# Other places in the line for scores, shifts, half-precision copies and value products in a decoder layer

## The reference

```python
scores = softmax(einsum('bhse,bhte->bhst', q, k) * scale, axis=-1)
att = einsum('bhst,bhte->bhse', scores, v)
x = layernorm(x + att.reshape(b, s, h * e) @ wo.T + bo)
# recurrence over t, elementwise in the 256 columns
out = A + exp(u + kk) * (vv * Bm + max(t - 1, 0))
A, Bm = exp(-w) * A + inc * exp(kk) * vv, exp(w) * Bm + inc * exp(-kk)
x = layernorm(x + out)
G, I = top_k(softmax(x @ Wg.T), 128)            # 128 of 128 tokens: all of them
h1 = gelu(ex @ W1[e] + b1[e])                   # 256 -> 1024
x = layernorm(x + sum_e G * (h1 @ W2[e] + b2[e]))
```

## Time and profile before

| | |
|---|---|
| median of 3 runs | 946.9 us (945.4 to 947.71) |
| the profiled execution, its own time | 947.15 us |
| its span, first to last instruction | 945.4 us |
| PE busy | 878.2 us, 93% |
| DVE busy | 596.7 us, 63% |
| ACT busy | 580.3 us, 61% |
| POOL busy | 79.1 us, 8% |
| granted clock of PE, mean | 0.968 of full speed |

### The profile page before, as it was taken

How to read it: one execution, slowest core, us unless ns; L and a number is a source line. 1 busy time by engine, 2 the same in 40 slices (tenths; PEclk the granted TensorE clock), 3 DMA queues, 4 the chain that set the end, 5 groups by cost and what they waited for, 6 DMA issues and landing times. The chain is left out here.

```text
span 945.4 us, 17487 instructions
## 1 busy us (share of the span) xinstructions
PE 878.2 (93%) x6480; PEld 799.0 (85%) x6480; DVE 596.7 (63%) x1222; ACT 580.3 (61%) x967; POOL 79.1 (8%) x116
## 2 busy tenths in 40 slices
PE   4759888899998999999998999999998999999997
PEld 3659888689987989888987899888997999899997
DVE  5888779767656575655676564664756555433574
ACT  4438875776657466665567666664666665445684
POOL 2320012000110010100120001200110000000000
PEclk8669989999999999999999999999999999999999
DMA  7617998998747954676547864578537765665340
GB/s 225 208 49 249 367 365 295 295 292 267 235 134 200 257 175 144 151 197 216 189 126 199 223 189 146 146 201 225 170 130 201 179 203 166 192 195 162 118 136 12
DMA packets 195379, 185.00 MB, mean 196 GB/s; under 512 B 61896, under 2 KB 161504, under 8 KB 195296
## 3 DMA queue, kind: packets, MB, share of 16 engines
q1 hardware_dynamic: 195296, 183.88, 65.0%
HBM read 135.60 MB, written 35.65 MB: 181 GB/s over the span
## 5 line engine op out<-in xcount | busy, mean ns | idle before, releaser
L881 ACT ACTIVATE h_all<-up_ps,b_all 128x512 f32<-128x512 f32 (+1 forms) x296 | 182.2, 631 | 246.4 <-PE up_ps L540 244.7
L775 PE MATMUL down_ps<-w_hi,h_hi 128*128 128x256 f32 x1024 | 297.4, 290 | 13.7 <-DVE acc L1124 13.6
L938 DVE TENSOR_TENSOR h_lo<-h_all,h_hi 128x512 fp32r<-128x512 f32 x256 | 177.2, 692 | 195.3 <-ACT h_hi L872 194.9
L776 PE MATMUL down_ps<-w_lo,h_hi 128*128 128x256 f32 x1024 | 292.0, 285 | 0.0
L777 PE MATMUL down_ps<-w_hi,h_lo 128*128 128x256 f32 x1024 | 291.7, 285 | 0.0
L538 PE MATMUL up_ps<-x2t_hi,w_hi 128*128 128x512 f32 (+1 forms) x592 | 221.8, 375 | 6.1 <-ACT h_all L881 5.2
L775 PEld LDWEIGHTS down_ps<-w_hi,h_hi 128*128 128x128 f32 x1024 | 197.4, 193 | 23.5 <-issue 12.5
L540 PE MATMUL up_ps<-x2t_hi,w_lo 128*128 128x512 f32 (+1 forms) x592 | 217.1, 367 | 0.0
L539 PE MATMUL up_ps<-x2t_lo,w_hi 128*128 128x512 f32 (+1 forms) x592 | 216.4, 366 | 0.0
L776 PEld LDWEIGHTS down_ps<-w_lo,h_hi 128*128 128x128 f32 x1024 | 198.2, 194 | 6.9
L777 PEld LDWEIGHTS down_ps<-w_hi,h_lo 128*128 128x128 f32 x1024 | 197.9, 193 | 0.0
(11 more groups left out here) (195 smaller groups left out, 958.7 us busy)
## 6 DMA issues: line engine op xcount, KB each, us to landing
w_hi<-w_parts SPq DMA_DIRECT2D x200, 256.0 KB, 3.3
w_lo<-w_parts SPq DMA_DIRECT2D x200, 256.0 KB, 3.6
w_raw<-in_w_dram SPq DMA_DIRECT2D x96, 256.0 KB, 4.2
w_parts<-w_hi SPq DMA_DIRECT2D x64, 256.0 KB, 4.0
w_parts<-w_lo SPq DMA_DIRECT2D x64, 256.0 KB, 4.4
x_in<-in_x_dram SPq DMA_DIRECT2D x8, 256.0 KB, 4.0
ctx_sb<-in_ctx_dram SPq DMA_DIRECT2D x8, 256.0 KB, 3.9
out_dram<-acc SPq DMA_DIRECT2D x8, 256.0 KB, 2.3
```

What stands on the lines that cost most here:

```text
L775: nc.tensor.matmul(ps, hi, w2h[:, c, :], start=c == 0 and j == 0, stop=False, skip_group_check=True)
L776: nc.tensor.matmul(ps, hi, w2l[:, c, :], start=False, stop=False, skip_group_check=True)
L881: a = nc.scalar.activation(h_all[:, unit % HALL, k * wide:(k + 1) * wide], up_ps[unit % 2][:, k * wide:(k + 1) * wide], ACT.Gelu_apprx_tan ...
L938: return nc.vector.tensor_tensor(dst, src, hi.bitcast(F32), ALU.subtract)
```

## The change

Numbers in `STEADY` and in the third pair's table of `EARLY` are changed; no code is. For pairs 3 to 7: T_0 and T_1 one item later, S_2 and S_3 two, M_2 three and M_3 four, so that the last two score steps stand at the last D of a visit and the shifts at the two items behind it; W_0, E_2 and E_3 two later, T_2 three, W_1 one, T_3 four, W_2 two, W_3 four, ATT two, CTX, WO, NORM1, Y1, XEXP and REC_0 to REC_3 one. BACK and what follows stay. For pair 2: T_0, T_1, M_3, W_0, W_1, T_2 and T_3 one later, W_2 and W_3 two.

```diff
-          V_ADD: -59, V_SPLIT: -58, S_0: -57, M_0: -57, S_1: -57, M_1: -57, DIAG_1: -53, E_0: -52, E_1: -52, T_0: -51, T_1: -46,
-          S_2: -45, M_2: -45, S_3: -45, M_3: -45, E_2: -40, E_3: -40, W_0: -40, T_2: -39, W_1: -37, T_3: -34, W_2: -32, W_3: -28,
-          ATT: -24, CTX: -23, WO: -21, NORM1: -19, Y1: -18, XEXP: -18, REC_0: -18, REC_1: -16, REC_2: -14, REC_3: -13,
+          V_ADD: -59, V_SPLIT: -58, S_0: -57, M_0: -57, S_1: -57, M_1: -57, DIAG_1: -53, E_0: -52, E_1: -52, T_0: -50, T_1: -45,
+          S_2: -43, S_3: -43, M_2: -42, M_3: -41, W_0: -38, E_2: -38, E_3: -38, T_2: -36, W_1: -36, T_3: -30, W_2: -30, W_3: -24,
+          ATT: -22, CTX: -22, WO: -20, NORM1: -18, Y1: -17, XEXP: -17, REC_0: -17, REC_1: -15, REC_2: -13, REC_3: -12,
...
-     S_0: 37, M_0: 37, S_1: 37, M_1: 37, DIAG_1: 40, E_0: 41, E_1: 41, T_0: 42, T_1: 46, S_2: 48, M_2: 48, S_3: 48, M_3: 48, W_0: 52, E_2: 53, E_3: 53, T_2: 54, W_1: 53,
-     T_3: 59, W_2: 60, W_3: 64, ATT: 68, CTX: 69, WO: 71, NORM1: 73, Y1: 76, XEXP: 76, REC_0: 76, REC_1: 77, REC_2: 79,
+     S_0: 37, M_0: 37, S_1: 37, M_1: 37, DIAG_1: 40, E_0: 41, E_1: 41, T_0: 43, T_1: 47, S_2: 48, M_2: 48, S_3: 48, M_3: 49, W_0: 53, E_2: 53, E_3: 53, W_1: 54, T_2: 55,
+     T_3: 60, W_2: 62, W_3: 66, ATT: 68, CTX: 69, WO: 71, NORM1: 73, Y1: 76, XEXP: 76, REC_0: 76, REC_1: 77, REC_2: 79,
```

## The result

The changed kernel takes 936.4 us (median of 4 runs, 935.67 to 936.93) beside 947.3 for the kernel before in the same comparison: a ratio of 0.988, 95% interval 0.985 to 0.991. The profiled execution took 936.91 us, its span is 935.2 us. For pairs 3 to 7 that distance runs from the first matmul of the item at offset -48 to that of the item at -32; the waits at U of -46, at D of -40 and at W_0 lie inside it.

The account below looks back on a forecast made before the run. PE bounds the kernel, with waits for gelu and accumulation in pairs 3 to 7. Gains of 7.7 (waits), 2.8 (clock) and 1.0 (pair 2), 11.5 us off 947.15, give 935.6 us; 8-in-10 range 931.0 to 941.5.

Parts of the forecast that it names:

- U's wait at -46: Pairs 3 to 7: with T_0 later, PE's U no longer waits for the gelu; 0.92 us gained there.
- The wait for the accumulation at -40: Pairs 3 to 7: DVE accumulates before M_2, so PE's D waits 0.2 us instead of 2.1.
- The new wait at W_0: Pairs 3 to 7: W_0 waits for M_3, 1.6 to 1.9 us; net gain 1.55 a pair, 7.7 in all.
- T_0 sets it one for one: Pairs 3 to 7: T_0's copy 2.03 us later moves T_1 along, 5.88 us behind it, and M_3's end one for one.
- rival 3: T_0's transposes land late, T_0 to T_1 taking 8.85 us instead of 5.88: 8.9 us slower, 956.1 us; chance 0.05.
- The clock: Pairs 4, 6, 7: one of three clock drops, 1.41 us each, is left; 2.8 us gained, bounds +4.2 to -2.8.
- Pair 2: Pair 2: W_0's wait of 0.97 us for M_3 falls to 0.3; 1.0 us gained, bounds 0 to 2.5.
- Everything behind at nothing: Pairs 3 to 7, E_2, E_3 and later steps: moves cost 0 us, bounds +0.5 to -2.5.
- The margin at item 277: Recurrence: D's margin behind the accumulation of item 275 falls from 1.4 to about 0.1 us; if gone, up to 0.5 a pair.
- The table load has no tail: ACT before T_0's copy: the table switch costs its 1.28 us load alone, the next activation 0.01 us behind.
- rival 4: The table load ahead of T_0's copy has a tail, 6.4 us in five pairs: 942.0 us; chance 0.02.

Follow-up runs that it names:

- pair 2 back: Changed kernel with pair 2's table of `EARLY` as before the change: 937.9 us, ratio 0.987 to the kernel before.
- scores and shifts alone: Kernel before with only S_2, S_3 at -43, M_2 at -42 and M_3 at -41 in pairs 3 to 7: 948.5 us, ratio 0.998.
- T moves alone: Kernel before with only T_0 and T_1 of pairs 3 to 7 one item later (-50, -45): 961.5 us, ratio 1.014.
- W_0 back: Changed kernel with W_0 of pairs 3 to 7 at -40 instead of -38: 963.4 us, ratio 1.015 to the kernel before.
- scores, shifts and W_0 alone: Kernel before with S_2, S_3 at -43, M_2 -42, M_3 -41 and W_0 -38 in pairs 3 to 7: 931.2 us, ratio 0.980.

## Why the prediction was right, step by step

- **U's wait at -46** (0.92 a pair): gone, as said.
- **The wait for the accumulation at -40** (2.1 to 0.2): gone in pairs 3, 4, 6 and 7; 0.54 is left in pair 5.
- **The new wait at W_0** (1.6 to 1.9): 1.42, 1.43, 1.44, 1.50 and 1.62 us by the rows of the five pairs, ended by the last shift. The place and the cause were right. A row counts idle time from the modelled end of the matmul before and shows less than the wait costs: by the distance of items it is 1.66 in pair 4, at the low end of what I had (the two times of the sum, 517.0 and 515.2, give 1.8 for pair 5, not 1.9).
- **T_0 sets it one for one:** shown by pair 5. Its interval from T_0 to T_1 came out at 504.30 - 497.41 = 6.89 us instead of 5.88, the others at 5.65 to 5.74. The last shift ended 16.86 us behind T_0's copy there and 15.63 in pair 4, where the interval was 5.65. Pair 5 gained 0.6 us (18.54 for 19.14) where I had 1.55. The missing 1.0 is the longer transfer. It is the mechanism of rival 3, in one pair of five and with 1.0 us instead of 3.0.
- **The clock** (one drop of three left): none is left in pairs 3 to 7, so 1.4 us more than the sum had. Over the study, as granted clock and idle rows show: waits of 1.4 to 1.6 us at W_0, no drop in fifteen (changed kernel twice, pair 2 back); 2.41 us, in two pairs of five (scores and shifts alone); over 4 us, in all ten (T moves alone, W_0 back). The kernel before had drops in three of five at 1.85 to 2.13. Which pair has the drop isn't settled by length alone: the five waits of 2.41 are alike, and a wait of 1.63 in pair 2 (below) was followed by one. That no drop is left was half luck then: I had no way to tell none from one. The drop's cost in pair 4, 1.41 by the earlier trace rows, agrees: items 173 to 189 took 29.4 us before and 26.4 after, 3.0 less, where pair 3, which had no drop, gained 1.5: 1.5 for the drop.
- **Pair 2** (1.0 gained): this step failed. D in item 45 did get its banks sooner, as the accumulation stood ahead of T_0's low copy, but the turned gates, which ACT makes in its order, came no sooner:

```profile
173.16 0.49 PE L718 MATMUL bank<-b_all,gate_t 24*128 24x256 f32 x2 [1.63 <-ACT gate_t L865]
```

  (idle 0.23 there before.) That D waited 2.08 instead of 3.48 and W_0's 0.97 is gone, but the idle time of 0.25 us and more between items 45 and 109 adds up to 6.8 us after and 6.7 before: the waits changed their places. In this trace a clock drop follows the row above, 0.83 over the ten us from 172, and items 45 to 109 take 1.05 us more. Over all traces the two sets of places can't be told apart, so its worth is 0 within about 1 us.
- **Everything behind at nothing:** right; the experiment with scores, shifts and W_0 alone shows that those moves carry no gain. The margin at item 277 held:

```profile
559.42 1.65 DVE L1124 SCALAR_TENSOR_TENSOR acc<-down_ps,gate,acc 128x256 f32<-128x256 f32 x4
...
560.49 0.36 PE L775 MATMUL down_ps<-w_hi,h_hi 128*128 128x256 f32 x1
```

  The first bank is free at 559.42 + 0.87 + 0.1 = 560.4 and D starts at 560.49: 0.1 us, as worked out, against 1.4 before.
- **The table load has no tail:** 495.52 + 1.28, gelu at 496.82, and T_0's copy 0.59 behind it. The 1380 ns of drain that the Trainium skill states ("ScalarE: Activation LUTs", What ACT_TABLE_LOAD costs) isn't seen in this place either; rival 4, which had such a tail, put the kernel at 942.0.

The sum: pairs 3 to 7 gained 1.5, 3.0, 0.5, 2.9 and 3.0 us between the items at offsets -48 and -32, 10.9 in all; pair 2's stretch lost 1.05; 0.4 was gained ahead of the first visit and is scatter; together 10.3, and the profiled executions differ by 947.15 - 936.91 = 10.24. I had 7.7 + 2.8 + 1.0 = 11.5. The errors, pair 5 (1.0 too much), pair 2 (1.0 promised, 1.05 lost in this trace) and the clock (1.4 too little), cancel in part: the number was closer than its terms. It also depends on the comparison: on another chip the same two kernels stood 15.4 us apart, 4 more than I had. Which part of the kernel before takes longer there isn't known, for no trace of it was taken on that chip.

## What to carry to other kernels

Where every engine walks one list in order, a step's place decides what stands ahead of what on each of them: look for short work that the bound engine waits for (four accumulations) behind long work that it doesn't need yet (eight reductions and shifts), and swap them; then look who waits for the long work, and move that too, or the wait only changes its name. Undoing one move at a time is cheap, and it showed that five of the moved numbers carry the gain, that the move of T_0 and T_1 cost a part of it (4.3 us in pairs 3 to 7 by the traces), and that two more items for W_0 and W_2 gave half as much again (7.8 on 15.4 us).

## What the runs showed of the hardware

- Idle time on PE and the granted clock, in pairs 3 to 7: no drop in fifteen waits of 1.4 to 1.6 us, three in five of 1.85 to 2.13, two in five of 2.41, ten in ten of over 4 us, always to the lower level. I had expected length to decide more sharply. Pair 2 shows that 1.6 us isn't safe in itself: the wait of 1.63 for the turned gates, with one of 2.08 about 4 us ahead of it, was followed by a drop in four of the seven traces with pair 2's new places; the single wait of 3.48 with the old ones in four of five.
- A pair of DMA transposes took 5.6 to 5.8 us from the copy to the next one in pairs 3, 4, 6 and 7, once 7.4 (pair 4, T_0 and T_1 alone), but 6.6 to 7.4 in pair 5 in all eight traces with T_0 at -50, and 5.7 to 5.9 there in the four with T_0 at -51. What it meets in that place isn't settled.
- Rows that name "issue" before a matmul can hide a plain semaphore wait: the last shift ended 0.10 us before it in pair 5.
